# A gated cross-attention and expert block: gate moved to ScalarE and GpSimd, similarity steps in PSUM, first batch in a group of its own, loops unrolled

## The chip, the cores and the metric

The kernel runs on 1 core of one Trainium2 chip. The metric is the device time of one execution in microseconds (us). The time before is 257.56 us, the median of 3 runs (257.23 to 257.66). In this text PE is the matmul engine TensorE, PEld its weight loads, DVE is VectorE, ACT is ScalarE, POOL is GpSimd and SP is the engine that issues the transfers. L700 is line 700 of the kernel before.

## The reference, cut to what matters

```python
# x, ctx: (16, 128, 1024); weight: (128, 128, 3); router_w (8, 1024); A (8, 16, 1024); Bm (8, 1024, 16)
def xattn(feature, embedding, weight):            # per batch: C = 128 channels, T = 1024
    emb_l = pad(embedding[:, :, :-1], left=1); emb_r = pad(embedding[:, :, 1:], right=1)
    sim = stack([cos(embedding, emb_l), cos(embedding, embedding), cos(embedding, emb_r)], axis=1)
    att = repeat(sim, C, axis=1)                  # (B, 3*C, T)
    inp = stack([f_pad[:, :, k:k + T] for k in range(3)], axis=2).reshape(B, C * 3, T)
    return einsum('bit,oi->bot', inp * att, weight.reshape(O, C * 3))
def ffn(x, router_w, router_b, A, Bm):            # x as 2048 rows of 1024
    probs = softmax(x @ router_w.T + router_b)    # 8 experts, the best 2 are kept
    topv, topi = top_k(probs, 2); gates = topv / sum(topv)
    h = einsum('nd,erd->ner', x, A)               # 16 hidden values per expert
    return einsum('ner,eor->no', h * w[:, :, None], Bm) * 0.5     # w: gates at topi
x = x + tanh(g_xattn) * xattn(layernorm(x), ctx, weight)
x = x + tanh(g_ffn) * ffn(layernorm(x), router_w, router_b, A, Bm)
```

## The kernel before

A batch is a tile of 128 partitions by 1024 columns; there are 16. Each goes through this pipeline, and each engine has a program of its own, written out by hand and tied to the others by semaphores. An engine executes its program strictly in order.

**The similarities, per group of four batches.** For each `ctx` batch ACT squares it (L461) and DVE or POOL multiplies neighbouring columns (L708, L343). `sum_context` (L920) sums both over the partitions with a one-hot weight, one PSUM row set per batch of the group. When four batches are in, ACT copies the sums out (L467), PE turns them round (`transpose_context`, L927), and DVE runs a chain of small instructions on 128 x 32 values: `context_columns` (L625, L627), the inverse square root by three Newton steps in `inverse_norms` (L636 to L648), the products in `similarities` (L658 to L666; PE's `next_norms`, L934, gives the neighbour's norm) and the split into three bf16 parts in `split_similarities` (L672 to L684). All of these operands lie in SBUF, apart from the two that PE has just written. PE turns the parts into rows (L941), and ACT copies them to `rows` (L471, L476). The chain for group g + 1 is dealt out, instruction by instruction, between the other DVE work of group g.

**The convolution, per batch in six steps.** A step i is a half h = i // 3 of the columns and a tap k = i % 3. PE spreads the similarity over the channels (`spread_similarities`, L953, banks 0 and 1 in turn), DVE multiplies it with the normalized feature (`modulate`, L700, result `pt`), and the tap is multiplied with its weights into bank 2 or 3. There are two ways to do this. A *split* tap has ACT round `pt` to `pt_hi` (L507) and POOL compute `pt_lo` (L368), and PE makes three fp32r matmuls (L969 to L971). A *whole* tap has PE make an fp32 matmul of `pt` itself, two instructions in the trace (L965). Whole are all six of the first batch and four of the 24 of each group (`WHOLE`), so there are 22 whole and 74 split taps. `LEAD` = 2: spreading runs four steps and modulation two steps ahead of the tap.

**The expert part.** DVE adds x (`residual`, L716), takes statistics (L722, L731), and POOL makes the inverse deviation (L394, L396). PE transposes the result (L980), multiplies with the expert weights (`experts_in`, L995), ACT copies hidden values and logits to SBUF (L527). DVE computes the logit (L740), the eight largest and their places (L744, L748), the distance to the largest (L747), and, after an exponential on ACT (L520), the gate in five instructions (L755, L758, L764, L768, L773, a batch later). POOL scales the hidden values (L377), PE transposes them (L1004), ACT makes two copies (L534, L535), POOL the remainder (L388), PE multiplies with the output weights (`experts_out`, L1014 to L1018, through one bank), DVE adds (`finish`, L780), and SP stores.

**The loops.** The body is one group of four batches. Each engine runs it for the first group, then twice in a hardware loop, then for the last group. Ahead of the first tap stand the four `sum_context` of group 0 and one whole similarity chain.

```python
WHOLE = ((), (4,), (4,), (3, 4))
LEAD = 2
...
                    for i in range(6):
                        if not (last and j + (i + 2 + LEAD) // 6 == G):
                            spread_similarities(*shifted(g, j, i, 2 + LEAD))
...
                        tap(g, j, i)
```

## Time and profile before

| what | value |
|---|---|
| time, median of 3 runs | 257.56 us (257.23 to 257.66) |
| span of the profiled execution | 256.0 us |
| time outside that span, by the three runs | 1.2 to 1.7 us (median run: 1.56 us) |
| PE, DVE, ACT, POOL busy | 216.1, 213.1, 157.2, 155.2 us |
| mean granted TensorE clock | 0.933 of full speed |

The profiled execution has no time of its own beside its span; what lies around the span is taken from the timed runs. An engine is busy while an instruction of it runs; a busy PE counts matmuls that overlap once. The granted clock is the share of the full 2.4 GHz at which PE ran.

### The profile page before, as it was taken

To read this page: it belongs to the slowest core of one execution; us is meant where nothing else is said; L and a number is where in the kernel's file an instruction comes from. 1 tells how busy PE (TensorE), PEld (TensorE's weight loads), DVE (VectorE), ACT (ScalarE), POOL (GpSimd) and SP (SyncE) were. 2 spreads that over 40 slices of the span, in tenths; PEclk is the share of its full clock that TensorE was granted. 3 is DMA by queue.
4 is the path that set the end of the run, shared out by engine and by line. 5 is a ranking of instruction groups with operands and counts; after the bars stand their busy time and mean duration, and the time that the engine had idled before them with its cause. 6 is when DMAs were issued, how large, how long until landed. Compare 5 with 4: busy or idle time off the path is not lost.

```text
span 256.0 us, 4267 instructions
## 1 busy us (share of the span) xinstructions
PE 216.1 (84%) x1080; PEld 136.3 (53%) x1080; DVE 213.1 (83%) x481; ACT 157.2 (61%) x283; POOL 155.2 (61%) x225
## 2 busy tenths in 40 slices
PE   6755999976995999896995999996998979697983
PEld 5133236554763546574753546573756656565761
DVE  2545686999989899999789899999789996979674
ACT  3668749664676678753686778753587765533320
POOL 2014558939376998846276998846267956745321
PEclk9996599998899999996899999996799988989999
DMA  6999106151221307171220304031222202020206
GB/s 205 333 293 387 59 0 188 63 186 64 82 82 21 147 0 292 40 286 43 82 86 10 154 0 154 10 105 59 82 82 81 83 1 83 3 82 0 82 3 247
DMA packets 8769, 27.24 MB, mean 106 GB/s; under 512 B 1616, under 2 KB 2128, under 8 KB 8752
## 3 DMA queue, kind: packets, MB, share of 16 engines
q1 hardware_dynamic: 8752, 27.05, 29.2%
q8 instruction: 7, 0.11, 0.2%
q14 instruction: 10, 0.08, 0.1%
HBM read 18.65 MB, written 8.39 MB: 106 GB/s over the span
## 4 chain that ended last, share of the span: by engine, by line
DVE 38%; PE 24%; issue 20%; POOL 7%; ACT 5%; DMA 2%; DVEq 1%; SPq 0%; ACTq 0%; POOLq 0%
DVE pt L700 7%; DVE pick L755 4%; DVE logit L740 4%; PE bank L965 4%; PE bank L995 3%; DVE bn L722 3%; PE bank L920 3%; POOL pt_lo L368 3%; DMA et<-ctx 2%; DVE below L747 2%; PE bank L980 2%; DVE x L716 2%; PE bank L953 2%; DVE pr L708 2%; POOL rs L396 2%
## 5 line engine op out<-in xcount | busy, mean ns | idle before, releaser
L368 POOL TENSOR_TENSOR pt_lo<-pt,pt_hi 128x512 fp32r<-128x512 f32 x74 | 96.3, 1304 | 33.2 <-ACT pt_hi L507 25.0
L700 DVE TENSOR_TENSOR pt<-xn,bank 128x512 f32<-128x512 f32 x96 | 64.9, 679 | 12.1 <-PE bank L953 6.9
L507 ACT ACTIVATE pt_hi<-pt 128x512 fp32r<-128x512 f32 x74 | 46.3, 627 | 36.1 <-DVE pt L700 35.6
L953 PE MATMUL bank<-rows,sel 96*128 96x512 bf16 (+1 forms) x96 | 39.6, 414 | 13.2 <-DVE pt L700 12.0
L969 PE MATMUL bank<-pt_hi,w_hi 128*128 128x512 f32 x74 | 37.1, 502 | 0.0
L995 PE MATMUL bank<-aT,xT 128*128 128x136 f32 x256 | 35.8, 284 | 0.0
L513 ACT ACTIVATE xT<-bank 128x512 f32<-128x512 f32 x32 | 18.9, 591 | 26.4 <-PE bank L980 26.4
L953 PEld LDWEIGHTS bank<-rows,sel 96*128 96x128 bf16 x96 | 9.5, 100 | 46.3 <-DVE pt L700 23.4
L995 PEld LDWEIGHTS bank<-aT,xT 128*128 128x128 f32 x256 | 33.5, 193 | 0.9 <-ACT xT L513 0.4
L970 PE MATMUL bank<-pt_lo,w_hi 128*128 128x512 f32 x74 | 30.3, 410 | 0.0
L971 PE MATMUL bank<-pt_hi,w_lo 128*128 128x512 f32 x74 | 30.2, 408 | 0.0
L980 PE MATMUL bank<-ident,x 128*128 128x128 f32 x128 | 21.2, 291 | 7.7 <-DVE x L716 7.7
L716 DVE TENSOR_TENSOR x<-bank,xt 128x512 f32<-128x512 f32 x32 | 22.0, 688 | 4.9 <-PE bank L971 4.2
L965 PE MATMUL bank<-pt,wT 128*128 128x512 f32 x44 | 25.9, 675 | 0.0
L980 PEld LDWEIGHTS bank<-ident,x 128*128 128x128 f32 x128 | 16.2, 149 | 14.5 <-DVE x L716 10.0
L920 PE MATMUL bank<-sq,onehot 128*32 128x512 f32 x64 | 20.8, 746 | 1.8 <-DVE pr L708 1.8
L780 DVE TENSOR_TENSOR x<-bank,x 128x512 f32<-128x512 f32 x32 | 21.2, 666 | 0.9 <-PE bank L1018 0.7
L489 ACT ACTIVATE unread<-xt,minus_mean 128x1024 f32<-128x1024 f32 x16 | 18.4, 1148 | 5.6 <-POOL minus_mean L348 5.6
L722 DVE BATCH_NORM_STATS2 bn<-x 128x6 f32<-128x512 f32 x32 | 21.7, 677 | 0.0
L920 PE MATMUL bank<-pr,onehot 128*32 128x512 f32 x64 | 20.8, 747 | 0.0
L461 ACT ACTIVATE sq<-et 128x1024 f32<-128x1024 f32 x16 | 16.8, 1048 | 5.9 <-DMA et<-ctx 4.9
L498 ACT ACTIVATE xn<-xt,offset,rs 128x1024 f32<-128x1024 f32 x16 | 19.7, 1229 | 0.6 <-POOL offset L359 0.6
(100 smaller groups left out, 386.3 us busy)
## 6 DMA issues: line engine op xcount, KB each, us to landing
et<-ctx SPq DMA_DIRECT2D x16, 512.0 KB, 5.8
xt<-x SPq DMA_DIRECT2D x16, 512.0 KB, 3.3
out<-x SPq DMA_DIRECT2D x15, 512.0 KB, 2.6
aT_in<-expert_aT SPq DMA_DIRECT2D x1, 544.0 KB, 9.4
bm_in<-expert_b SPq DMA_DIRECT2D x1, 512.0 KB, 9.9
out<-x SPq DMA_DIRECT2D x2, 256.0 KB, 2.0
sel<-select SPq DMA_DIRECT2D x1, 288.0 KB, 10.5
wT_in<-conv_wT SPq DMA_DIRECT2D x1, 192.0 KB, 10.0
```

The costliest lines, as they stand in the source:

```text
L368: nc.gpsimd.tensor_tensor(pt_lo[:, i, :], pt[:, i, :], pt_hi[:, i, :], ALU.subtract).then_inc(lo_done, 1)
L507: nc.scalar.activation(pt_hi[:, i, :], pt[:, i, :], ACT.Copy).then_inc(hi_done, 1)
L700: nc.vector.tensor_tensor(pt[:, i, :], xn[:, j % 2, h * HALF + k:(h + 1) * HALF + k], sim_ps[i % 2][:, :], ALU.mult).then_inc(mod_done, 1)
L722: nc.vector.bn_stats(bn2[:, j % 2, 6 * h:6 * h + 6], x1[:, j, half(h)]).then_inc(bn2_done, 1)
L920: last = nc.tensor.matmul(sum_ps[32 * q:32 * q + 32, :], onehot[:, j, :], src[:, j % 2, half(q % 2)], start=(j == 0), stop=(j == G - 1))
L953: nc.tensor.matmul(sim_ps[i % 2][:, :], sel[:, j, k, :], rows[:, g, half(h)], start=True, stop=True).then_inc(spread, 1)
L965: nc.tensor.matmul(conv_ps[h][:, :], wT[:, k * P:(k + 1) * P], pt[:, i, :], start=(k == 0), stop=(k == TAPS - 1)).then_inc(tap_done, 1)
L969: nc.tensor.matmul(conv_ps[h][:, :], w_hi[:, k, :], pt_hi[:, i, :], start=(k == 0), stop=False)
L970: nc.tensor.matmul(conv_ps[h][:, :], w_hi[:, k, :], pt_lo[:, i, :], start=False, stop=False)
L971: nc.tensor.matmul(conv_ps[h][:, :], w_lo[:, k, :], pt_hi[:, i, :], start=False, stop=(k == TAPS - 1)).then_inc(tap_done, 1)
L980: last = nc.tensor.transpose(xT_ps[:, c * P:(c + 1) * P], x1[:, j, h * HALF + c * P:h * HALF + (c + 1) * P], ident[:, :])
L995: last = nc.tensor.matmul(h_ps, xT[:, j % 2, c, :], aT[:, c, :], start=(c == 0), stop=(c == KC - 1))
```

## The change

Nearly every function is rewritten, and the loops over groups are unrolled into a loop over the batches n = 0 to 15 at build time. What an engine does in step (n, i) is now read from tables. The parts:

1. **Gate.** The exponential, the distance and the five DVE instructions go. ACT computes the second weight as sigmoid(second - first) from the two largest logits (`second_weight`). POOL builds the gate in six small instructions (`weigh_experts`). The logit reads its main operand from PSUM rather than from the copy in SBUF. The copy `hwT` goes (one ACT instruction), and the remainder `hwT_lo` moves from POOL to DVE with one PSUM operand; the transposed hidden values lie in the output bank.
2. **Similarity chain.** The chain's long-lived values stay in free columns of the PSUM bank that holds the turned sums; guess, rinv, dr and the bf16 parts remain in SBUF. The copy L625 goes. The order of the four sums in the bank changes to suit.
3. **Groups** are (0), (1, 2, 3), then three of four. So there are five chains instead of four. Group 1's chain is run in batch 0. Loads are reordered: x 0 comes before ctx 1.
4. **Lead.** Modulation is three steps and spreading five steps ahead of the tap, from batch 1 on (one and three in batch 0).
5. **Taps.** In each batch from 1 on, steps 2 and 5 are whole, the other four split: 36 whole and 60 split in all.
6. **Small moves.** The mean is scaled in the ACT instruction that sums (POOL's L348 goes). `rows` 0 to 63 are copied by DVE in every group. Products: eight on DVE, eight on POOL (ten and six before).

```diff
-WHOLE = ((), (4,), (4,), (3, 4))
-LEAD = 2
+WHOLE = (2, 5)
+GROUPS = ((0,), (1, 2, 3), (4, 5, 6, 7), (8, 9, 10, 11), (12, 13, 14, 15))
+TURNS = {(1, 3): 2, (5, 3): 3, (9, 3): 4}
+NEIGHBOURS = {(0, 2): 1, (2, 3): 2, (6, 3): 3, (10, 3): 4}
+ROWS = {(0, 3): 1, (3, 0): 2, (7, 0): 3, (11, 0): 4}
+ON_POOL = (2, 3, 5, 7, 9, 11, 13, 15)
...
+        def ahead(m):
+            lead = 3 if m >= STEPS else 2 if m == STEPS - 1 else 1
+            return min(m + lead, M - 1)
...
+            def weigh_experts(n):                                    # POOL
+                i = n % 2
...
+                pool.wait_ge(topi_done, n + 1)
+                nc.gpsimd.tensor_copy(topf[:, i, :], topi[:, i, 0:2]).then_inc(topf_done, 1)
+                pool.wait_ge(w2_done, n + 1)
+                nc.gpsimd.tensor_tensor(g2[:, i:i + 1], w2[:, i:i + 1], rs2[:, i:i + 1], ALU.mult).then_inc(g2_done, 1)
+                pool.wait_ge(g2_done, n + 1)
+                nc.gpsimd.tensor_tensor(g1[:, i:i + 1], rs2[:, i:i + 1], g2[:, i:i + 1], ALU.subtract).then_inc(g1_done, 1)
+                pool.wait_ge(topf_done, n + 1)
+                nc.gpsimd.tensor_scalar(gb[:, i, :], ids[:, :], topf[:, i, 1:2], g2[:, i:i + 1], ALU.is_equal,
+                                        ALU.mult).then_inc(picked, 1)
+                pool.wait_ge(g1_done, n + 1)
+                nc.gpsimd.tensor_scalar(ga[:, i, :], ids[:, :], topf[:, i, 0:1], g1[:, i:i + 1], ALU.is_equal,
+                                        ALU.mult).then_inc(picked, 1)
+                pool.wait_ge(picked, 2 * (n + 1))
+                nc.gpsimd.tensor_tensor(gate[:, i, :], ga[:, i, :], gb[:, i, :], ALU.add).then_inc(gate_done, 1)
...
+            def second_weight(n):                                    # ACT
+                nc.scalar.activation(w2[:, i:i + 1], top[:, i, 0:1], ACT.Sigmoid, bias=top[:, i, 1:2],
+                                     scale=-1.0).then_inc(w2_done, 1)
...
+            def inverse_norms(q):                                    # DVE
+                s = columns(q)                                       # the PSUM bank of the sums
+                n_all, guess_n, excess = s[:, :, 4:8], s[:, :, 8:12], s[:, :, 12:16]
...
-                nc.vector.scalar_tensor_tensor(out=logit[:, :], in0=hs[:, j % 2, ER:ER + E],
-                                               scalar=rs2[:, j % 2:j % 2 + 1], in1=rb[:, :],
+                nc.vector.scalar_tensor_tensor(out=logit[:, i, :], in0=h_ps[:, ER:ER + E], scalar=rs2[:, i:i + 1],
+                                               in1=rb[:, :], op0=ALU.mult, op1=ALU.add).then_inc(logit_done, 1)
...
+            def hidden_rest(n):                                      # now DVE
+                nc.vector.tensor_tensor(hwT_lo[:, i, :], hwT_ps(n), hwT_hi[:, i, :].bitcast(F32),
+                                        ALU.subtract).then_inc(hwT_rest, 1)
...
+            sum_context(0)                                           # PE, ahead of the loop
+            transpose_context(0)
+            sum_context(1)
+            next_norms(0)
+            sum_context(2)
             transpose_similarities(0)
+            sum_context(3)
+            for k in steps_at(-1, 2):
+                spread_similarities(k)
+            transpose_context(1)
+            for n in range(B):
+                for i in range(STEPS):
+                    if (n, i) in ROWS:
+                        transpose_similarities(ROWS[n, i])
+                    for k in steps_at(m, 2):
+                        spread_similarities(k)
+                    if i == 0 and n >= 3:
+                        experts_out(n - 3, 0)
+                    if i == 1 and n >= 1:
+                        transpose_tokens(n - 1, 1)
+                    if i == 2 and n >= 1:
+                        experts_in(n - 1, 0)
+                    if i == 2 and n >= 3:
+                        experts_out(n - 3, 1)
+                    if i == 3 and n >= 1:
+                        experts_in(n - 1, 1)
+                    if i == 4 and n >= 2:
+                        transpose_hidden(n - 2)
+                    if i == 5:
+                        transpose_tokens(n, 0)
...
+                    tap(m)
```

## Rows read from the trace of the kernel before

**Rows 1.** The page: span, and busy time of each engine.

```profile
span 256.0 us, 4267 instructions
PE 216.1 (84%) x1080; PEld 136.3 (53%) x1080; DVE 213.1 (83%) x481; ACT 157.2 (61%) x283; POOL 155.2 (61%) x225
```

**Rows 2.** Windows: stretch, length, busy per engine, clock, DMA share, GB/s.

```profile
36.00:244.00 208.00, 182.56 (x936) 120.36 (x932) 187.14 (x420) 133.00 (x247) 141.33 (x191) 0.94 0.23 84
120.00:124.00 4.00, 4.00 (x13) 2.81 (x12) 2.77 (x12) 1.11 (x2) 0.17 (x1) 0.50 0.00 0
```

**Rows 3.** Waits: who waited for whom; us in total, times, longest.

```profile
PEld bank L953 <- DVE pt L700: 23.4, 26, 3.1
PE bank L934 <- DVE rinv L648: 8.4, 4, 2.2
```

**Rows 4.** Timeline: start, us, engine, line; one stretch of POOL and DVE.

```profile
92.50 1.29 POOL L368 TENSOR_TENSOR pt_lo<-pt,pt_hi 128x512 fp32r<-128x512 f32 x1
92.76 1.07 DVE L755 TENSOR_SCALAR pick<-ids,topi 128x8 f32<-128x8 f32 x1
```

**Rows 5.** Single lines of DVE: ns minimum/median/maximum, first and last start.

```profile
L740 DVE SCALAR_TENSOR_TENSOR logit<-hs,rs,rb x16: 215/980/1234, 45.3 to 247.2; 128x8 f32<-128x8 f32 x16
L700 DVE TENSOR_TENSOR pt<-xn,bank x96: 660/678/689, 24.7 to 237.2; 128x512 f32<-128x512 f32 x96
```

**Rows 6.** Groups of instructions: busy us, mean ns; then idle before.

```profile
L740 DVE SCALAR_TENSOR_TENSOR logit<-hs,rs,rb 128x8 f32<-128x8 f32 x16 | 12.8, 801 | 8.1 <-ACT hs L527 6.5 <-POOL rs L396 1.4
L755 DVE TENSOR_SCALAR pick<-ids,topi 128x8 f32<-128x8 f32 x16 | 12.3, 767 | 0.0
L747 DVE TENSOR_SCALAR below<-logit,top 128x8 f32<-128x8 f32 x16 | 8.4, 522 | 0.1
L773 DVE TENSOR_SCALAR gate<-expk,einv,rs 128x8 f32<-128x8 f32 x16 | 7.6, 474 | 0.0
L758 DVE SCALAR_TENSOR_TENSOR pick<-ids,topi,pick 128x8 f32<-128x8 f32 x16 | 6.6, 413 | 0.5
L764 DVE SCALAR_TENSOR_TENSOR expk<-expo,pick 128x8 f32<-128x8 f32 x16 | 5.4, 339 | 0.0
L648 DVE SCALAR_TENSOR_TENSOR rinv<-excess,guess 128x32 f32<-128x32 f32 x4 | 3.8, 961 | 0.0
L662 DVE TENSOR_TENSOR sim<-dr,bank 128x64 f32<-128x64 f32 x4 | 0.9, 220 | 0.6 <-PE bank L935 0.5
L708 DVE TENSOR_TENSOR pr<-et 128x1023 f32<-128x1023 f32 x10 | 14.1, 1408 | 6.5 <-DMA et<-ctx 5.6 <-PE bank L920 0.8
```

**Rows 7.** The chain that ended last: start, us, PE's pieces back to back.

```profile
238.12 0.93 PE bank L995 x8
239.04 0.23 PE bank L969
...
239.85 1.77 PE bank L965 x4
...
242.33 0.44 PE bank L980 x4
```

**Rows 8.** Windows 36 to 244, matmuls of L920 alone: PE and PEld busy.

```profile
sum 208.00, PE 10.73 PEld 1.57; mean PE 10.73 PEld 1.57
```

**Rows 9.** The chain that ended last: start, us, the stretch before batch 0.

```profile
9.04 5.38 PE bank L920 x24
...
24.68 0.70 DVE pt L700
```

**Rows 10.** Timeline of DVE: the residual's second half of batches 0 and 15.

```profile
39.02 0.69 DVE L716 TENSOR_TENSOR x<-bank,xt 128x512 f32<-128x512 f32 x1
...
243.49 0.69 DVE L716 TENSOR_TENSOR x<-bank,xt 128x512 f32<-128x512 f32 x1 [1.56 <-PE bank L971]
```

**Rows 11.** Groups of instructions of POOL and ACT, as rows 6.

```profile
L368 POOL TENSOR_TENSOR pt_lo<-pt,pt_hi 128x512 fp32r<-128x512 f32 x74 | 96.3, 1304 | 33.2 <-ACT pt_hi L507 25.0 <-PE bank L971 8.0
L507 ACT ACTIVATE pt_hi<-pt 128x512 fp32r<-128x512 f32 x74 | 46.3, 627 | 36.1 <-DVE pt L700 35.6
L348 POOL TENSOR_TENSOR minus_mean<-xsum,minus_t 128x1 f32<-128x1 f32 x16 | 3.7, 232 | 11.9 <-ACT unread L483 11.9
L461 ACT ACT_TABLE_LOAD x1 | 1.3, 1283 | 0.7 <-PEq L1140 0.7
```

More of the change, by code:

```diff
@@ L29, in flamingo_kernel @@
     B, C, T = x.shape
-    NG = B // G
     KC = T // P
@@ L238, in parts_before, with whole, parts_up_to @@
-        def parts_before(g, j, i):
-            count = [6 - len(steps) for steps in WHOLE]
-            return sum(count) * g + sum(count[:j]) - count[0] + sum(m not in WHOLE[j] for m in range(i))
-        def past(g, j, k):
-            return not isinstance(g, int) or G * g + j >= k
+        SETUP = 11
         def half(h):
             return slice(h * HALF, (h + 1) * HALF)
+        def whole(k):
+            return k < STEPS or k % STEPS in WHOLE
+        def parts_up_to(k):
+            return sum(not whole(m) for m in range(k + 1))
@@ L316, in _ @@
+            for n in range(B - 4, B - 1):
+                store(n)
             for h in range(2):
@@ L440, in body @@
                                                 ALU.subtract).then_inc(bm_lo_done, 1)
[L441 to L453 removed]
+            weigh_experts(B - 2)
@@ L593, in body @@
                         nc.scalar.activation(bm_hi[:, :], bm[:, :], ACT.Copy).then_inc(bm_hi_done, 1)
-                    high(3)
-                    if one:
-                        logits_evacuate(*before(1))
-                    high(4)
-                    if two:
-                        hidden_evacuate(*before(2))
-                    if stats:
-                        feature_squares(*ahead)
-                    if j == 1 and not last:
-                        sums_evacuate(g + 1)
-                    high(5)
@@ L605, in body @@
-                    if j == 0 and not last:
-                        square(g + 1, 2)
-                    if one:
-                        exponent(*before(1))
-                    tokens_evacuate(g, j, 0)
-            each_group(act, body)
-            tokens_evacuate(NG - 1, G - 1, 1)
-            logits_evacuate(NG - 1, G - 1)
-            hidden_evacuate(NG - 1, G - 2, last_hwT_ps[0])
-            exponent(NG - 1, G - 1)
-            hidden_evacuate(NG - 1, G - 1, last_hwT_ps[1])
+                    if i == 5:
+                        tokens_evacuate(n, 0)
@@ L781, in finish, with some @@
                                         ALU.add).then_inc(out_done, 1)
+            def some(of, count):
+                for _ in range(count):
+                    next(of, None)
             nc.vector.memset(rows[64:96, :, 0:1], 0.0).then_inc(setup, 1)
-            dve.wait_ge(setup, 11)
-            for j in range(G):
-                next_product(0, j)
-            context_columns(0)
+            dve.wait_ge(setup, SETUP)
+            product(0)
+            product(1)
             for _ in inverse_norms(0):
@@ L871, in body @@
-                    residual(g, j, 0)
-                    steps(roots)
-                    steps(picks)
-                    steps(roots)
-                    ahead(5)
-                    steps(roots)
-                    steps(picks)
-                    steps(roots)
-                    token_stats(g, j, 0)
-                    if j == 2 and not last:
-                        similarities(g + 1)
-                        parts = split_similarities(g + 1)
-                        steps(parts)
@@ new lines, in _ @@
+                    some(norms, 1)
+                    some(sims, 1)
+                    if i == 3:
+                        residual(n, 0)
+                    if i == 5 and n >= 2:
+                        hidden_rest(n - 2)
+                    if i == 5:
+                        some(picks, 1)
+                    if i == 4:
+                        token_stats(n, 0)
+                    if i == 5:
+                        some(norms, 1)
+                        some(picks, 1)
+                        some(sims, 1)
+                        some(picks, 1)
@@ L1098 @@
+            experts_out(B - 3, 0)
+            transpose_tokens(B - 1, 1)
+            experts_in(B - 1, 0)
+            experts_out(B - 3, 1)
+            experts_in(B - 1, 1)
+            transpose_hidden(B - 2)
+            experts_out(B - 2, 0)
+            experts_out(B - 2, 1)
+            transpose_hidden(B - 1)
+            experts_out(B - 1, 0)
+            experts_out(B - 1, 1)
 def kernel(x, ctx_4096, g_xattn, g_ffn, L0_xattn_weight, L0_ffn_router_w, L0_ffn_router_b, L0_ffn_A, L0_ffn_Bm):
```

1073 lines of the change are left out of this document (458 added, 615 removed).

## The prediction

> **What bounds the kernel now.** I read four views. The page's first lines say which engines can matter at all: PE and DVE are both busy for more than 210 of 256.0 us, ACT and POOL for some 155 [rows 1]. That doesn't separate PE from DVE, so I took the steady stretch, windows 36 to 244: DVE 187.1, PE 182.6 of 208 us [rows 2]. Then the waits: the entries of PE there name DVE, its multiplication L700 above all, and at the group's end the last Newton step L648 [rows 3]. So PE waits for DVE. Part of PE's busy time is also no work: in the windows there are stretches such as 120 to 124 at a clock of 0.50, the lower of the two levels (1.2 GHz), and the mean is 0.94 [rows 2]. That one comes after PE had waited for L648.
>
> The last view tells why DVE is full. The timeline shows the 128x8 comparison L755 start at 92.76 and end at 93.83, while POOL's L368 runs from 92.50 to 93.79 [rows 4]: eight columns take a microsecond because the instruction ends only when POOL's has. The single lines say the same of L740 (215 ns at best, 980 at the median), but not of L700, which has one operand in PSUM and stays within 660 to 689 in 96 executions, although POOL runs L368 under most of them [rows 5]. So DVE's small instructions with SBUF operands are held by POOL, and those with a PSUM operand aren't.
>
> The steady part runs from the second residual of batch 0 (39.0) to that of batch 15 (243.5): 204.5 us, 13.6 per batch. 12.5 us follow it [rows 10].
>
> **Step 1, DVE's work.** The gate's lines that go cost 12.3 + 8.4 + 7.6 + 6.6 + 5.4 = 40.3 us [rows 6]. The logit stays, with PSUM as its main operand: 12.8 falls to 16 x 0.215 = 3.4, so 9.4 less [rows 5, 6]. The chain's L648 falls from 3.8 to 4 x 0.22 = 0.9 by the PSUM row L662, 2.9 less; its other held instructions I leave out. Two products fewer: 2.8 less [rows 6]. Added: `hidden_rest`, 128 columns with a PSUM operand, lies between L662 (0.22, 64 columns) and L700 (0.68, 512 columns); I take 0.3, near the first, 16 times: 4.8 (ends 3.5 and 10.9). A fifth chain of some 22 small instructions at 0.22: 4.8. Four more copies of `rows`, each taken as one L700: 2.7. Sum: 213.1 - 55.4 + 12.3 = 170 us. Of the 43 us some 40 lie in the steady part: 147 instead of 187, 9.8 per batch.
>
> The Trainium skill (SBUF: State Buffer, "Who interferes with whom") says that VectorE and GpSimd share a port pair as an exclusive lock, and that a VectorE instruction with at most one SBUF input, outside the two-port modes, doesn't take it. By that rule the two rows on L755 and L740 are the lock, and the new chain and gate are free of it. It doesn't say whether the per-partition scalar of the logit counts as an input.
>
> I bound that from rows: if the logit is held as before, DVE keeps the 9.4 us and stands at 179, still under PE.
>
> **Step 2, PE's work.** At full clock, pieces back to back are: one 512-column fp32r pass 0.23, a whole tap 1.77 / 2 = 0.89, half of `experts_in` 0.93, four token transposes 0.44 [rows 7]. Per batch from 1 on: six spreads 1.4, four split taps 12 x 0.23 = 2.8, two whole taps 1.8, `experts_in` 1.9, `experts_out` 1.4, transposes 0.9 and 0.1: 10.3 us. Fifteen batches: 155. Ten `sum_context` of 10.73 / 10 each [rows 8] add 10.7; three groups' turns, each about three times the four transposes, add 4. Together 170 us, 11.3 per batch. By the same prices the old mix (74 split, 16 whole taps) is 166: the change costs PE 4 us, since a whole tap takes 0.89 against 0.69.
>
> So PE had 166 us of work at full clock in 204.5: 38.5 us were waits and slow clock. With DVE at 9.8 and PE at 11.3 per batch, PE is the bound. Of the 38.5 the waits on DVE and the slow stretches behind them should mostly go; the deeper lead (three steps instead of two) helps as well, since a split tap passes DVE, ACT and POOL (0.68 + 0.63 + 1.30, [rows 5, 11]) within three steps of 1.9 us. I keep a quarter, 10 us: PE's program still depends on DVE's residual and additions twice per batch. Ends: nothing kept, or two thirds (25). Steady part: 170 + 10 = 180 us.
>
> **Step 3, POOL and ACT.** POOL: 14 fewer `pt_lo` are -18.3, six small gate instructions 16 times at the 0.232 of L348 are +22.3 [rows 11]: 155.2 becomes 159, at most 10 per batch; the six are covered by PE's 11.3. ACT: 14 fewer `pt_hi` at 0.627, -8.8; one small sigmoid against one exponential. Both hidden. Unrolling alone I cost at nothing; no row prices it.
>
> **Step 4, the start.** With batch 0 alone in its group the first chain need not wait for the other three `sum_context`, which now end at 9.04 + 5.38 = 14.4 [rows 9]. But DVE takes product 1 first, whose load now comes behind x 0, and PE's list puts `sum_context` 1, 2 and 3 between the chain's stages; number 3 waits for an ACT square that stands behind the copy of `rows`. Of the 4.2 us that could be won (a start of the chain near 10.2) I keep 1: the first modulation near 23.7 instead of 24.68 [rows 9]. Batch 0 then contains group 1's whole chain, and its taps 3 to 5 wait for it; but its taps are no slower than now. I put its second residual at 37.5 instead of 39.0; ends: 34.8 (all 4.2 won) and 43 (chain of 22 x 0.22 = 5 us uncovered). The end after batch 15 keeps its 12.5: the gate there is a serial chain on POOL rather than DVE, 0 to 1 us longer.
>
> **Sum.** 37.5 + 180 + 12.5 = 230 us of span against 256.0. The runs' median lies 1.56 above the profiled span, so 231.5 us.
>
> **Rivals.**
> - *A, in-order coupling (0.20).* DVE, ACT and POOL have room, but their programs and PE's wait for each other at fixed places: the one output bank is now also used for the transposed hidden values, so `transpose_hidden` waits for an addition on DVE one and a half steps after its matmuls. Then more than half of the 38.5 stays, 20 to 27 us: 241 to 249. For it: now too DVE isn't full (187 of 208). Against: the waits name DVE.
> - *B, POOL's gate becomes the bound, slower (0.04).* The trace shows no comparison with two per-partition scalars on POOL. The nearest rows are L348 (0.23) and L368 (1.30), the ends. POOL has 8.5 us per batch without the six; it reaches today's 13.6 if each takes 0.85. At 1.0 the steady part is 15 x 14.5 = 217, the time 269. Everything behind them on POOL, `hidden` and the next `pt_lo`, is late, and PE waits for `pt_lo`.
> - *C, sigmoid reloads tables (0.03).* One table load of 1.28 us serves the whole kernel now [rows 11]. If the sigmoid needs another table than the copies around it, there are two loads per batch: 41 us on ACT, 157 - 9 + 41 = 189, and its bursts delay `pt_hi`: some 240 to 260.
> - *D, the DVE relief isn't the limit (0.03).* All 38.5 stays: 37.5 + 170 + 38.5 + 12.5 + 1.56 = 260.
>
> On C, the Trainium skill (ScalarE: Activation LUTs, "Table sets: the hidden batching unit") says that tanh is in the sigmoid's set too and that cheap functions are in every set; by that there is one load or two in all. Its price for a switch is 2.66 us with the drain, by which two switches per batch would cost 85 us on ACT, an estimate, and the kernel would be slower. The one load seen for tanh, exponential and copies agrees as far as it goes.
>
> **Chances and range.** The forecast, steady part kept to between 0 and 18 us above PE's sum, has 0.70: 221 to 240. The range goes from 221 to 245 and takes in the nearer half of A; outside are its rest, B, D, part of C and a better start. Slower by over 0.2% is B, D and a part of C, 0.06; within 0.2%, about what a measurement here can tell from no change, 0.01; faster 0.93.
>
> **What would show it.** Right: L740's successor near 0.22 us in all executions; DVE busy near 170; 15 batches in about 180 us; the clock above 0.96; PE over 90% busy in the steady part. Wrong: POOL's six instructions above 0.5 us each, more than two table loads, PE waits for `hwT_rest` or the output bank, or the first modulation after 25 us. The prediction falls if PE's idle and slow time stays above 25 us.

## The result, and the profile after

The changed kernel takes 261.15 us (median of 4 runs, 259.4 to 261.96) against 257.39 us for the kernel before beside it. The ratio is 1.0173, 95% interval 1.0104 to 1.0242: slower, by 4 us. The forecast was 231.5 us, so it missed by 30 us and had the wrong sign. The runs of one kernel differ by up to 3%, so all ratios here, and the column "undisturbed" of the table further down, leave out each run that lies more than some 1.5% above the fastest of its kernel. In this part L-numbers without a word are those of the changed kernel.

First the page of the changed kernel, against [rows 1].

```profile
span 260.0 us, 3722 instructions
PE 215.1 (83%) x1082; PEld 135.8 (52%) x1082; DVE 167.3 (64%) x403; ACT 144.5 (56%) x253; POOL 155.2 (60%) x277
```

DVE lost 45.8 us of work (170 us were forecast, 167.3 came), and yet the span grew. Next the groups of instructions that answer to [rows 6, 11]: busy us, mean ns.

```profile
L676 DVE SCALAR_TENSOR_TENSOR logit<-bank,rs,rb 128x8 f32<-128x8 f32 x16 | 3.5, 217 | 0.0
L593 DVE TENSOR_TENSOR bank<-bank,guess 128x32 f32<-128x32 f32 x15 | 3.0, 198 | 0.4
L691 DVE TENSOR_TENSOR hwT_lo<-bank,hwT_hi 128x128 fp32r<-128x128 f32 x16 | 4.6, 285 | 2.5 <-ACT hwT_hi L505 2.4
L379 POOL TENSOR_SCALAR gb<-ids,topf,g 128x8 f32<-128x8 f32 x16 | 8.5, 533 | 0.0
L382 POOL TENSOR_SCALAR ga<-ids,topf,g 128x8 f32<-128x8 f32 x16 | 6.3, 393 | 0.0
L497 ACT ACT_TABLE_LOAD x1 | 1.3, 1283 | 0.0
```

The prices of the instructions came out as forecast: the logit and the chain are held no more, the remainder costs 0.285 us, POOL's comparisons are in the mean below the 0.85 us at which they would matter (two single executions of L379 took 1.44 us), and the sigmoid loads its table once. So the loss isn't in what the instructions cost. The windows, against [rows 2]: the steady part from the second residual of batch 0 to that of batch 15, its last four batches, and a stretch of low clock.

```profile
49.50:246.30 196.80, 174.99 (x908) 114.75 (x907) 137.61 (x329) 117.44 (x214) 136.72 (x234) 0.97 0.27 89
205.70:246.30 40.60, 39.84 (x209) 28.56 (x208) 31.16 (x69) 22.76 (x46) 29.71 (x58) 1.00 0.22 78
121.00:124.00 3.00, 2.96 (x8) 1.55 (x8) 2.13 (x12) 1.40 (x3) 1.00 (x5) 0.50 0.02 5
```

The last four batches take 10.15 us each with PE 98% busy at full clock; PE's prices had said 10.3. The steady part as a whole takes 196.8 us where 180 were forecast, and it begins at 49.5 where 37.5 were (timeline of DVE, the rows that answer to [rows 10]):

```profile
49.50 0.69 DVE L659 TENSOR_TENSOR x<-bank,xt 128x512 f32<-128x512 f32 x1 [0.23 <-PE bank L841]
...
246.27 0.69 DVE L659 TENSOR_TENSOR x<-bank,xt 128x512 f32<-128x512 f32 x1 [0.79 <-PE bank L841]
```

So of the 29.6 us that were missed the start has 12.0, the steady part 16.8 and the tail 1.2 (260.0 - 246.3 = 13.7 against 12.5); the profiled execution lies 0.4 above the median. Against the kernel before, the sign has two parts: the steady part is 7.7 us shorter (196.8 against 204.5), but the start, which now holds two chains instead of one, is 10.5 us longer (49.5 against 39.0) and the tail 1.2, together the 4.0 us by which the spans differ. With the start of before the kernel would have been faster by some 6 us, an estimate from these rows. Where the steady part's went, the waits say (in total, times, longest), against [rows 3]:

```profile
PEld bank L827 <- DVE pt L652: 49.1, 63, 3.7
PE bank L827 <- DVE pt L652: 24.7, 25, 2.2
...
DVE bank L616 <- PE bank L809: 18.5, 5, 5.5
...
DVE bank L581 <- PE bank L802: 16.4, 5, 5.9
...
DVE rows L639 <- PE bank L815: 10.0, 5, 2.9
...
DVE x L659 <- DMA out<-x: 4.0, 3, 3.4
```

PE still waits for DVE's multiplications, although DVE is busy for only 137.6 of the 196.8 us. And DVE waits for PE at three places of the similarity chain, five times each, once per chain: 45 us together, 32 of them in the chains of groups 2 to 4 (the timeline of each). Of such waits the kernel before had this one (waits, before), beside some below 1.3 us:

```profile
DVE nd L625 <- PE bank L927: 3.6, 1, 3.6
```

One chain, first on DVE and then on PE (timelines), shows how the two belong together:

```profile
116.47 0.20 DVE L581 TENSOR_SCALAR bank<-bank 128x32 f32<-128x32 f32 x1 [4.68 <-PE bank L802]
...
131.97 0.23 DVE L616 TENSOR_TENSOR bank<-dr,bank 128x64 f32<-128x64 f32 x1 [3.82 <-PE bank L809]
139.21 0.68 DVE L639 COPY rows<-bank 64x1024 bf16<-64x1024 bf16 x1 [2.14 <-PE bank L815]
```

```profile
119.06 0.39 PE L827 MATMUL bank<-rows,sel 96*128 96x512 bf16 x1 [1.92 <-DVE pt L652]
121.04 0.61 PE L827 MATMUL bank<-rows,sel 96*128 96x512 bf16 x1 [0.78 <-DVE pt L652]
...
134.20 0.39 PE L827 MATMUL bank<-rows,sel 96*128 96x512 bf16 x1 [1.49 <-DVE pt L652]
...
140.55 0.39 PE L827 MATMUL bank<-rows,sel 96*128 96x512 bf16 x1 [1.37 <-DVE pt L652]
```

PE spreads two steps ahead of DVE's multiplication, so a DVE that isn't full can get up to two steps of its program ahead of PE's. At L581 it needs the sums that PE turns in the same step of its program, and stands 4.68 us, since it can't pass over that instruction. Its multiplications for the next taps stand behind it, so when it goes on it is level with PE, and now PE waits for it: PE stands for 1.92 us until 119.06, then for 0.78, and the clock falls to 0.50 in the windows (121 to 124: the lower level, 1.2 GHz). From second residual to second residual, the six batches in which DVE reads a result of PE (1, 2, 5, 6, 9, 10) take 15.0 to 16.7 us. Without chains and with the store ahead of the loads (run b3 below) they take 9.6 to 12.4. Batches 3, 7 and 11 to 14 take 10.5 to 10.8 in both. Batches 4 and 8 are longer for another reason: PE makes three `sum_context` in each, and they take 13.7 us in b3 as well.

The last wait of the list is another thing. The diff has one line of SyncE's program that the prediction passed over as "loads are reordered":

```diff
 # batch n of SyncE's program: load_x(n + 3), loads of ctx, then
-  store(n - 3)
+  store(n - 4)
```

SyncE's timeline, and DVE's with the second addition of batch 0 (L696), after which the store could go, and the first residual of batch 4 (L659), which needs the buffer:

```profile
82.28 11.14 SPq L274 DMA_DIRECT2D xt<-x  x2
93.52 1.20 SPq L269 DMA_DIRECT2D et<-ctx  x2
94.77 0.42 SPq L278 DMA_DIRECT2D out<-x  x1
```

```profile
87.53 0.68 DVE L696 TENSOR_TENSOR x<-bank,x 128x512 f32<-128x512 f32 x1
...
102.53 0.69 DVE L659 TENSOR_TENSOR x<-bank,xt 128x512 f32<-128x512 f32 x1 [3.44 <-DMA out<-x]
```

The data was ready at 88.2. The store went out at 94.8, behind a load of x that waited for the residual of batch 3 (the second of the two in the first line; by itself it starts at 93.10), and behind two ctx loads, and DVE stood for it 3.44 us.

### The profile page after: what moved, and what is told of

Its sections match the earlier page's. It is cut to its first block, busy times and chain, and to the rows that moved or that the text cites. A ratio compares the mean times of both kernels' runs of the same rounds, so it can differ in the third digit from the quotient of the medians.

```text
span 260.0 us, 3722 instructions
## 1 busy us (share of the span) xinstructions
PE 215.1 (83%) x1082; PEld 135.8 (52%) x1082; DVE 167.3 (64%) x403; ACT 144.5 (56%) x253; POOL 155.2 (60%) x277
## 4 chain that ended last, share of the span: by engine, by line
PE 55%; DVE 18%; issue 10%; DMA 8%; POOL 4%; ACT 2%; SPq 0%; POOLq 0%; DVEq 0%; ACTq 0%
PE bank L841 11%; PE bank L866 10%; DVE pt L652 7%; PE bank L827 7%; DMA out<-x 6%; PE bank L855 4%; PE bank L795 4%; PE bank L845 3%; PE bank L846 3%; PE bank L847 3%; DVE bn L664 2%; DMA xt<-x 2%; PE bank L884 2%; PE bank L885 2%; PE bank L886 2%
## 5 line engine op out<-in xcount | busy, mean ns | idle before, releaser
L357 POOL TENSOR_TENSOR pt_lo<-pt,pt_hi 128x512 fp32r<-128x512 f32 x60 | 76.9, 1283 | 52.6 <-ACT pt_hi L478 52.4
L652 DVE TENSOR_TENSOR pt<-xn,bank 128x512 f32<-128x512 f32 x96 | 63.7, 669 | 6.1 <-PE bank L827 5.3
L478 ACT ACTIVATE pt_hi<-pt 128x512 fp32r<-128x512 f32 x60 | 37.5, 627 | 50.6 <-DVE pt L652 50.5
L827 PE MATMUL bank<-rows,sel 96*128 96x512 bf16 x96 | 39.3, 414 | 24.8 <-DVE pt L652 24.7
L841 PE MATMUL bank<-pt,wT 128*128 128x512 f32 x72 | 42.7, 679 | 0.0
L659 DVE TENSOR_TENSOR x<-bank,xt 128x512 f32<-128x512 f32 x32 | 22.0, 687 | 14.8 <-PE bank L841 10.7
L696 DVE TENSOR_TENSOR x<-bank,x 128x512 f32<-128x512 f32 x32 | 21.8, 680 | 11.5 <-PE bank L886 11.5
L845 PE MATMUL bank<-pt_hi,w_hi 128*128 128x512 f32 x60 | 28.4, 474 | 0.0
L795 PE MATMUL bank<-sq,onehot 128*32 128x512 f32 x64 | 19.7, 694 | 6.3 <-ACT sq L438 3.1
L846 PE MATMUL bank<-pt_lo,w_hi 128*128 128x512 f32 x60 | 24.0, 400 | 0.0
L847 PE MATMUL bank<-pt_hi,w_lo 128*128 128x512 f32 x60 | 23.9, 399 | 0.0
L344 POOL TENSOR_TENSOR ve<-squares,eps_t 128x1 f32<-128x1 f32 x16 | 4.2, 260 | 27.8 <-ACT unread L462 27.8
```

The costliest lines, as they stand in the source:

```text
L357: nc.gpsimd.tensor_tensor(pt_lo[:, i, :], pt[:, i, :], pt_hi[:, i, :], ALU.subtract).then_inc(lo_done, 1)
L478: nc.scalar.activation(pt_hi[:, i, :], pt[:, i, :], ACT.Copy).then_inc(hi_done, 1)
L652: nc.vector.tensor_tensor(pt[:, i, :], xn[:, n % 2, h * HALF + t:(h + 1) * HALF + t], sim_ps[k % 2][:, :], ALU.mult).then_inc(mod_done, 1)
L795: last = nc.tensor.matmul(sum_ps(q)[32 * r:32 * r + 32, :], onehot[:, b, :], src[:, :, r // 2, :], start=(b == 0), stop=(b == len(GROUPS[q ...
L827: nc.tensor.matmul(sim_ps[k % 2][:, :], sel[:, SLOT_OF[n], t, :], rows[:, q % 2, half(h)], start=True, stop=True).then_inc(spread, 1)
L841: nc.tensor.matmul(conv_ps[h][:, :], wT[:, t * P:(t + 1) * P], pt[:, i, :], start=(t == 0), stop=(t == TAPS - 1)).then_inc(tap_done, 1)
```

## The experiments

The table holds what all runs are compared by. "Start" is the begin of the second residual of batch 0, "steady" the time from there to that of batch 15, both from the timeline of DVE in the profiled execution (kernel before: [rows 10]). That execution is a single one, and its time stands beside them. "All" and "undisturbed" are medians; the last column has the ratio to the kernel before, with its 95% interval. Runs whose names begin with the same letter were made on the same chip, each letter's on another. The kernel before took 255.16, 255.28, 254.93 and 254.36 us (undisturbed) beside a, b, c and d, and 257.39 us (all) beside the changed kernel. The ratios differ from the quotients of these medians by up to 1.4%, so differences of a few us are read here from the undisturbed times, and across chips they carry an error of 1 to 2 us.

| kernel | start | steady | profiled | all | undisturbed (runs) | ratio |
|---|---|---|---|---|---|---|
| before | 39.0 | 204.5 | | 257.39 | | |
| changed | 49.5 | 196.8 | 261.57 | 261.15 | 261.15 (4) | 1.017 (1.010 to 1.024) |
| a1_norms_later | 48.5 | 189.9 | 254.65 | 255.88 | 250.59 (1) | |
| a2_all_later | 50.8 | 182.2 | 249.49 | 247.11 | 245.07 (2) | 0.954 (0.944 to 0.963) |
| a3_no_chain | 51.0 | 172.8 | 239.75 | 238.63 | 234.11 (1) | |
| a4_start | 42.4 | 196.0 | 253.70 | 253.14 | 253.14 (4) | 0.982 (0.972 to 0.991) |
| b1_store | 49.7 | 191.1 | 256.02 | 257.34 | 257.34 (9) | 1.008 (1.004 to 1.012) |
| b2_later_store | 50.5 | 176.7 | 242.51 | 241.11 | 241.11 (4) | 0.940 (0.934 to 0.946) |
| b3_no_chain_store | 49.4 | 165.4 | 230.07 | 230.09 | 230.09 (4) | 0.899 (0.893 to 0.905) |
| b4_later_store_start | 47.2 | 176.1 | 238.56 | 234.66 | 233.74 (5) | 0.916 (0.910 to 0.921) |
| c1_before_no_gate | 38.3 | 182.8 | 234.77 | 235.74 | 235.05 (4) | 0.924 (0.918 to 0.930) |
| c2_lead_two | 42.1 | 176.5 | 233.94 | 235.86 | 235.86 (5) | 0.926 (0.921 to 0.932) |
| c3_one_whole | 41.8 | 176.9 | 234.01 | 234.38 | 234.13 (3) | 0.920 (0.914 to 0.927) |
| c4_warm | 43.8 | 176.3 | 235.36 | 235.99 | 234.22 (3) | 0.916 (0.909 to 0.923) |
| d1_loads | 42.1 | 176.4 | 234.98 | 234.45 | 234.45 (4) | 0.909 (0.897 to 0.921) |
| d2_no_gate_late_store | 39.6 | 190.3 | 243.68 | 240.94 | 239.04 (2) | 0.931 (0.916 to 0.946) |
| d3_before_late_store | 39.5 | 208.9 | 262.67 | 260.90 | 257.95 (3) | 1.014 (1.003 to 1.025) |

**The handoffs (a1, a2, a3).** a1 starts DVE's part of the chain two steps later than PE turns the sums; a2 does the same at the two other places.

```diff
 # a1, DVE
 TURNS = {(1, 3): 2, (5, 3): 3, (9, 3): 4}                  # PE turns the sums; DVE no longer starts here
+NORMS_FROM = {(1, 5): 2, (5, 5): 3, (9, 5): 4}             # DVE alone
 # a2, besides
-NEIGHBOURS = {(0, 2): 1, (2, 3): 2, (6, 3): 3, (10, 3): 4}
+NEIGHBOURS = {(0, 2): 1, (2, 2): 2, (6, 2): 3, (10, 2): 4}   # PE
+SIMS_FROM  = {(0, 2): 1, (2, 4): 2, (6, 4): 3, (10, 4): 4}   # DVE
-ROWS = {(0, 3): 1, (3, 0): 2, (7, 0): 3, (11, 0): 4}
+ROWS = {(0, 3): 1, (2, 5): 2, (6, 5): 3, (10, 5): 4}         # PE
+ROWS_REST = {(0, 3): 1, (3, 1): 2, (7, 1): 3, (11, 1): 4}    # DVE; ACT at (3, 0), (7, 0), (11, 0)
 # a3
-TURNS = {...}; NEIGHBOURS = {(0, 2): 1, ...}; ROWS = {(0, 3): 1, ...}
+TURNS = {};    NEIGHBOURS = {(0, 2): 1};      ROWS = {(0, 3): 1}
```

Expected of a1:

> The changed kernel, but DVE begins the norm chain of groups 2 to 4 two steps after PE has turned the sums, rather than in the same step. Handoff theory (DVE runs ahead of PE, meets PE's result of the same step, stands still and loses its lead): the wait of some 5 us in front of the first chain instruction goes in three groups, 10 to 15 us less than 261, that is 246 to 251. Rival, the chain's own work on DVE and PE makes these batches long: no change, 259 to 262. Rival, the split of the taps, the gate on POOL or the deeper lead make them long: no change.

Expected of a2:

> As before, and the other two handoffs of groups 2 to 4 get room as well: PE makes the neighbour norms one step earlier and DVE begins the similarities two steps after that; PE turns the parts round one step earlier, ACT copies its rows one step and DVE its rows two steps after that. No work is left out. Handoff theory: the nine batches that now last 15.6 us fall to 12 or less, 225 to 235. Rival, the chain's own work: 255 to 262. Rival, taps, gate or lead: 255 to 262.

Expected of a3:

> The changed kernel without the similarity chains of groups 2 to 4 (turn, norms, neighbour norms, splitting, rows are left out; the batches 4 to 15 use rows left by the groups 0 and 1; sums over the context are still made). It bounds what chain and handoffs together can cost. Handoff theory: nine batches fall from 15.6 to about 11 us, 215 to 225, and the kernel with later handoffs comes within 10 us of it. Rival, the chain's own work: also 215 to 225, but far from the kernel with later handoffs. Rival, taps, gate or lead: stays above 245.

The direction is as the handoff theory said, the size isn't. The same work takes 6.9 us less in the steady part with one handoff moved, 14.6 with three; without the chains of groups 2 to 4 it takes 24.0 less. (The profiled executions of these three lie above the undisturbed times; b1 against b2 below, both within 1.4 us of theirs, gives the 14.4 us of the three handoffs again.) The four runs of a1 go from 250.59 to 257.3, so only the fastest lies in the theory's range. a2 is 16 us below the changed kernel by the undisturbed runs, and still above the range; so is a3, of which no run is below 234. DVE's waits in a2 (L620 and L643 there are L616 and L639 of the changed kernel; L700 is the addition, L663 the residual):

```profile
DVE x L700 <- PE bank L892: 20.4, 17, 2.2
...
DVE bank L620 <- PE bank L815: 9.4, 2, 6.5
DVE x L663 <- DMA out<-x: 7.1, 3, 3.9
...
DVE rows L643 <- PE bank L821: 3.7, 2, 2.9
```

The chain's waits of the three later groups are gone; only the two early chains have theirs. DVE's other waits for PE, at the addition, are those of an engine with time to spare. But the waits for stores grew, from 4.0 to 7.1 us here and 10.1 in a3, where batches 4 and 5 took 16.1 and 15.5 us without a chain. There was a second limit behind the first.

**The start (a4).** On PE, the chain's rows stand ahead of `sum_context(2)` and the first two spreads of batch 0 ahead of `sum_context(3)`, `expert_means` goes from step 1 of batch 0 to step 4, and `next_norms` ahead of `sum_context` in a step.

```diff
-sum_context(2); transpose_similarities(0); sum_context(3); spreads of steps 0 to 2
+transpose_similarities(0); sum_context(2); spreads 0 and 1; sum_context(3); spread 2
-if n == 0 and i == 1: expert_means()
+if n == 0 and i == 4: expert_means()
```

> The changed kernel with another order at the start only: on PE the parts of group 0 are turned round before the sums of context 2, two spreads stand before the sums of context 3, the expert means are made in step 4 of batch 0 instead of step 1 (the subtraction on DVE moves to batch 1), and the neighbour norms stand before the sums of the same step. Theory that the start lost its time to PE work placed in front of what DVE waits for: first modulation from 24.8 to about 20, second residual of batch 0 from 49.5 to 41 to 44, 5 to 8 us less in all, 253 to 256. Rival, the start is set by transfers: within 1 us of the changed kernel.

It came at 253.14: 8 us below the changed kernel, with the start at 42.4 instead of 49.5 and the steady part unchanged (196.0). The first multiplication, in the changed kernel and in this one (timeline of DVE, one fence each):

```profile
24.81 1.29 DVE L652 TENSOR_TENSOR pt<-xn,bank 128x512 f32<-128x512 f32 x2 [4.05 <-PE bank L827]
```

```profile
21.19 1.29 DVE L652 TENSOR_TENSOR pt<-xn,bank 128x512 f32<-128x512 f32 x2 [1.79 <-PE bank L827]
```

3.6 us are won there, and 3.4 more within batch 0, where group 1's chain waited 5.49 us at L616 in the changed kernel and 2.12 here. The clock isn't what made this start late: in b3, whose program is the same up to here, it was granted 1.00 in the window 9 to 25, against 0.50 in the changed kernel, and the second residual of batch 0 came at 49.4 all the same.

**The store (b1 to b4).** The store is put ahead of the loads: in the changed kernel (b1), in a2 (b2), in a3 (b3), and in a2 with a4's start (b4).

```diff
 for n in range(1, B):
+    if n >= 4: store(n - 4)
     if n + 3 < B: load_x(n + 3)
     ...                                        # loads of ctx
-    if n >= 4: store(n - 4)
```

> The changed kernel with one thing put back as before: SyncE issues the store of a finished batch ahead of the next load of x and of the ctx loads, instead of behind them (one batch later). In the profile of the changed kernel the residual L659 waited 4.0 us for stores, three times, the longest 3.4 at 102.5. Theory of the store: those waits go, and what PE lost behind them, 3 to 6 us in all: 255 to 258. Rival, that the similarity handoffs alone set the slow batches, so that the store's wait only moves to the next handoff: 259 to 262, with the same nine batches of some 15.6 us.

> The kernel with all handoffs a few steps later (247.1 us), with the store put back ahead of the loads. Its profile shows 7.1 us of waits of the residual for stores, three times, up to 3.9. Two limits in turn (theory now): with the handoffs moved the store is the next that holds DVE; taken away it gives 7 us and some of the lead lost behind each: 236 to 241. Rival, handoffs alone: the waits move elsewhere, 245 to 249. By both the start stays as it is, second residual of batch 0 near 50.5.

> The kernel without the chains of groups 2 to 4 (238.6 us; its output isn't the reference's), with the store put back ahead of the loads. Its profile still had slow batches: 16.1 and 15.5 us for batches 4 and 5, with 10.1 us of waits for stores. Theory (the store is the second limit): all batches from 3 on take 10.5 to 11, the second residual of batch 15 comes near 213, the time is 226 to 231. Rival (what is left is PE's own pace or the slow clock): 236 to 239.

> All three together: handoffs later, the store ahead of the loads, and PE's start put in another order (spreads of batch 0 ahead of two sums, the expert means three steps later). The start alone gave 8 us of 261. If the three add: 228 to 234, faster than the kernel before by 9 to 11%. If the start's gain is eaten because batch 0 and 1 wait for loads instead: 236 to 241.

All four medians fell within 0.7 us of the ranges of the theory of two limits, and outside the rivals'; for b1 that is weak, as its 257.34 lies only 2 us below the rival's range and its chip was the quicker by as much. The steady part shrinks by 5.7, 5.5 and 7.4 us (changed to b1, a2 to b2, a3 to b3; a2 and a3 by profiled executions that lie 4 to 6 us high), the undisturbed times by 3.8, 4.0 and 4.0, and no wait for a store is left in any of the four. The issues in the changed kernel and in b1 (KB each, median us from issue to landing, one fence each):

```profile
out<-x SPq DMA_DIRECT2D x15, 512.0 KB, 5.0
```

```profile
out<-x SPq DMA_DIRECT2D x15, 512.0 KB, 2.6
```

The store isn't only issued later in the changed kernel, it also takes twice as long to land when it goes out right behind the loads: the median is 4.9 us in a2, d2 and d3 too, and 2.6 in before, b2 and c1. In b3, where neither holds, this is what the steady batches are like (windows, 82 to 214):

```profile
82.00:214.00 132.00, 130.21 (x694) 86.38 (x693) 102.29 (x215) 86.28 (x163) 107.34 (x188) 1.00 0.27 100
```

PE is 99% busy at full clock. Its steady part, 165.4 us, is what step 2 had summed for PE less the three groups' turns that b3 leaves out: 170 - 4 = 166.

**DVE's relief by itself (c1).** The kernel before, with the gate's instructions left out of DVE. Schedule, store, lead, taps and chain are those of before.

```diff
-below = logit - top[0]; topi = max_index(...); pick0, pick, expk, esum, einv    # L747, L748, L755 to L768
-gate = expk * einv * rs2
+gate = ids * rs2
```

> The kernel before with the gate left out (output isn't the reference's): the largest's place L748, L747, L755, L758, L764, L768 and ACT's exponential go, and the gate is the expert numbers times the inverse deviation. DVE loses 12.3 + 8.4 + 6.6 + 5.4 + 1.3 + 2.4 + 2.5 + 1.3 = 40.2 of its 213.1 us; chain, lead, taps, groups and the store's place stay as before. What the prediction's step 2 said (DVE's relief alone gives back most of the 38.5 us of waits and slow clock): 228 to 234. Theory now (relief gives what DVE really held, and the chain's handoffs, where DVE arrives early, keep a part): 238 to 247. Rival D (DVE isn't the limit): 253 to 257.

235.74 us (235.05 undisturbed), a ratio of 0.924; the steady part goes from 204.5 to 182.8. That lies between the 228 to 234 of the prediction's step 2 and the theory's 238 to 247. Rival D is refuted: DVE was the limit, and relieving it in the old order is worth 20 us. The chain's handoffs cost little in the old order. DVE's waits for PE in it are short (L622 and L659 are the chain's first two places; L776 is the copy of `rows` ahead of batch 0, the only one that DVE makes there):

```profile
DVE nd L622 <- PE bank L908: 4.3, 3, 2.7
DVE sim L659 <- PE bank L916: 2.9, 1, 2.9
...
DVE rows L776 <- PE bank L922: 1.2, 1, 1.2
```

8.4 us in four chains, against 45 in the changed kernel's five. The programs say why. In the kernel before, PE turns the sums in step 5 of the group's second batch and DVE reads them in step 1 of the third, two steps later. PE makes the neighbour norms in step 4 and DVE reads them at the end of step 5. The rows of the later groups are copied by ACT alone. The change gave up these distances: its tables put each pair into one step, and DVE copies rows too. What the same-step order costs beside a full DVE was not run.

**Lead, mix of taps, clock, loads (c2, c3, c4, d1).** Each is b4 with one thing changed.

```diff
 # c2
-lead = 3 if m >= STEPS else 2 if m == STEPS - 1 else 1
+lead = 2 if m >= STEPS - 1 else 1
 # c3
-WHOLE = (2, 5)
+WHOLE = (5,)
 # c4, PE: 7 and 6 matmuls of 128 columns whose result isn't used, around the first next_norms
+for _ in range(7): matmul(conv_ps[0][:, 0:P], mean_w, mean_w)
 # d1, SyncE: selection matrix and weights ahead of ctx 2
-load_e(2); sel; wT
+sel; wT; load_e(2)
```

> The kernel with handoffs later, store and start (234.7 us), with a lead of two steps instead of three. If the third step of lead is what lets PE ride over DVE's stalls and the way of a split tap through DVE, ACT and POOL (0.67 + 0.63 + 1.28 us and the handoffs, within two steps of 1.75): 238 to 246. If two steps are enough: 233.5 to 236.

> The same kernel with one whole tap per batch from 1 on instead of two (15 more split taps): PE has 15 x 0.2 = 3 us less to do, ACT 15 x 0.63 = 9.4 and POOL 15 x 1.28 = 19.2 more (POOL 174 us, 10.9 per batch). If PE's work sets the pace: 231 to 232.5. If POOL's queue does, so that the mix of taps is part of the gain: 236 to 241.

> The same kernel with 13 idle matmuls (128 columns, results not used) on PE where it waits in the start: seven behind sum_context(1), six behind the first next_norms. In its profile the clock was at the lower level from 15 us on, the three sums in the start took 1.87 us each instead of 1.06, and the second residual of batch 0 came at 47.2, in the kernel with the start alone at 42.4. If the clock in the start is what differs: 43 or below, and 229 to 232 us. If the start waits on DVE's chain and on loads anyway: 234 to 236.

> The kernel with handoffs later, store and start (234.7 us), with the loads of the selection matrix and of the weights issued ahead of ctx 2. In its profile PE waited for the selection matrix until 14.5 us, and its second residual of batch 0 came at 47.2, in like kernels at 42 to 44. If the load is the rest of the start's delay: the first modulation 1 to 2 us earlier than 20.3 to 21.2, the second residual at 40 to 42, 232 to 234 us. If ctx 2, which now comes later, takes its place: 234 to 236.

None of the four does much: 234.1 to 235.9 us undisturbed against 233.7, steady parts within 0.8 us of each other. So the third step of lead is worth 2 us at most, and nothing in the steady part. The mix of taps is a wash within 0.8 us of the steady part: batches 12 to 14 take 10.4 us each with one whole tap against 10.5 with two, and the batches before them differ either way. The idle matmuls don't help. The start of b4 in its profile (47.2) was not that of its kind: a4, with the same program up to there, has 42.4, and c2, c3, c4 and d1, with nearly the same, have 41.8 to 43.8. The profiled execution of b4 is also 4.8 us above its kernel's undisturbed median. The windows 30 to 50 of b4 and of c2 show the granted clock at 0.67 and 0.95:

```profile
30.00:50.00 20.00, 18.28 (x76) 8.59 (x75) 11.06 (x20) 8.85 (x12) 9.19 (x8) 0.67 0.06 19
```

```profile
30.00:50.00 20.00, 18.07 (x102) 9.06 (x102) 12.63 (x23) 13.28 (x19) 11.89 (x11) 0.95 0.22 80
```

What decides that clock I can't say; c4 didn't settle it.

**The store's place by itself (d2, d3).** The kernels c1 and before, with the store one batch later as in the changed kernel.

```diff
-if j >= 3: store(g, j - 3)
-elif not first: store(g - 1, j + 1)
+if not first: store(g - 1, j)
```

> The kernel before with the gate left out (235.7 us; output isn't the reference's), with the store of a finished batch issued one batch later, behind the next load of x and the ctx loads, as in the changed kernel. There the store was issued 2.3 us after the first half's residual of the batch before, and the next residual wanted its buffer some 8 us later. If the store's place costs whenever the batches are short: waits of L713 for stores appear, 237.5 to 243. If only the changed kernel's own order (residual at step 3, its addition just ahead of it) makes it late: 234.5 to 236.5, no wait.

> The kernel before with the store's place alone moved one batch later. A batch takes 13.6 us there and the residual's first half comes some 9 us after the second half of the batch before. If a late store is hidden by a full DVE: 254.5 to 256.5, no change. If it costs on its own: 258 to 261.

Both theories that hid it were wrong: d2 239.04 against 235.05 of c1 (undisturbed, on two chips), d3 257.95 against 254.36 of before on the same chip, ratio 1.014 with an interval that excludes 1. The steady parts are 7.5 and 4.4 us longer, but both profiled executions are 4.6 us or more above their undisturbed medians, so the times are the better measure. The wait for stores appears in both; first d2, then d3:

```profile
DVE x L711 <- DMA out<-x: 4.5, 2, 2.7
```

```profile
DVE x L714 <- DMA out<-x: 5.5, 2, 3.5
```

The late store costs about 4 us even with a full DVE (d3). A likely reason, not tested apart: a full DVE is itself the limit, so a wait in its program is lost.

## Why the prediction was wrong, point by point

**Step 1, DVE's work: right.** 170 us forecast, 167.3 measured. The logit takes 217 ns in the mean and never more than 226, although in eight of its 16 executions POOL was in the middle of a 1.28 us `pt_lo` (L357); the Newton steps' L593 takes 198 ns. By the rule in the Trainium skill (SBUF — State Buffer, "Who interferes with whom"), cited there, VectorE instructions with at most one SBUF input, outside the two-port modes, don't take the lock; the rows agree. The logit has two SBUF operands beside the one in PSUM, a per-partition scalar and the bias row, so in this trace neither of them led to its being held.

**Step 3, POOL and ACT: right.** POOL 155.2 us (159 forecast), though partly by luck: the comparisons with two scalars took 0.39 and 0.53 us in the mean instead of 0.23, two more products were added, and the sum had forgotten that the remainder and the mean's scaling leave POOL. Rivals B and C are out: no bound on POOL, one table load for the sigmoid, two in all.

**Step 2, PE's work: the sum was right, what was kept of the waits was wrong.** PE's 170 us hold: b3 gives 165.4 without the turns. (One figure beside it was off: 14 taps more at 0.20 us each are 2.8 us, not 4.) The failed step is "I keep a quarter, 10 us". The changed kernel kept 196.8 - 170 = 27 us, above the 25 at which the prediction said it would fall. The runs show what the 27 are:

- 5.7 us the store's place (changed against b1). By the undisturbed times it is about 4 us, in this pair (3.8, across chips) as in a2 to b2, a3 to b3 and c1 to d2 (4.0 each) and in before to d3, on one chip (3.6). The prediction had the line in front of it and gave it no price.
- 14.4 us the three handoffs of the chain (b1 against b2, both on one chip; changed against a2 gives 14.6).
- What is left is 176.7 - 170 = 6.7 us (b2). That is what the forecast's 10 us stood for, and with both repaired they would have been enough. All of it is tied to the chains of groups 2 to 4, since b3, which lacks them, stands at its price.

Step 2's premise, that DVE's relief gives the waits back, was right in direction where it was made, and short in size: in the old order the relief is worth 21.7 us of the steady part (c1), where the forecast wanted back 28.5 of its 38.5. What it lacked was the question what the relieved engine would do in the new order. The table of steps has PE's turning and DVE's first use of it in the same step (1, 3), and likewise at the two other places. A DVE with room gets ahead of PE's program, by up to two steps, and then stands at a same-step handoff until PE has come up. In the old order, with one or two steps between PE's instruction and DVE's, a light DVE waits 8.4 us in all (c1); in the new one 45. Most of what the relief had gained in the steady part was paid back there and at the store.

**Step 2's lead: not borne out.** "The deeper lead helps as well": c2 shows nothing in the steady part and 2 us at most in the time.

**Step 4, the start: the second failed step, wrong by 12.0 us.** 37.5 forecast, 49.5 measured, above its upper end of 43. What failed is "but its taps are no slower than now", with group 1's chain priced as 5 us of DVE's small instructions and nothing for what DVE and PE wait for each other in it. The first multiplication came at 24.81 (23.7 forecast), so 1.1 us of it lie before. The rest lies in batch 0: its first tap starts as in the kernel before (27.24 us, before 27.22), its last at 48.43 against 37.96 (timelines of PE). a4 gives back 7.1 us, half of them by PE's order before batch 0 and half by the order within it. One cause was in the diff and missed: `expert_means` stood in PE's waits before batch 0 (2.3 us in two pieces) and now stands in batch 0's step 1 (3.15 us), with group 1's `next_norms` behind it. The other 4.9 us, down to 37.5, stay open; neither loads (d1) nor idle matmuls (c4) moved them.

**Rivals.** A had the right kind (engines that wait for each other at fixed places) and the wrong place: not the output bank or the residual, but the chain, and so the wrong price, 241 to 249. D had the right number, 260, by luck and for a wrong reason: the relief does count (c1), its gain went elsewhere. No rival said that a relieved engine in front of a handoff can lose again what its relief gains, and none had the start later than before.

The ledger in times: 261.15 to 233.74 us by the three repairs of b4, the work unchanged, 8.4% under the kernel before (ratio 0.916). 2 us above the forecast are left.

## What to carry to other kernels

When an engine that was full is relieved, look for each instruction on it that waits for another engine's result of the same step: it can now arrive early, stand, and lose the lead that the others live on. Give such handoffs as many steps as the engine can run ahead (two here, which took the waits away in a2 and b2), and look in the diff for distances that the old order had. Price the start by itself: here it turned a shorter steady part into a longer kernel. And read every line of the transfer queue's program in a diff: a store that moves behind a load inherits the load's wait, and the buffer it frees is late by as much.

## What the runs showed of the hardware

A store of 512 KB issued right behind loads landed after 5.0 us in the median, issued ahead of them after 2.6, in the same kernel (changed and b1).

Kernels with nearly the same start were granted 0.67 (b4) or 0.95 (c2) of the full clock in windows 30 to 50, and the second residual of batch 0 came 5 us apart; which of the two a run gets wasn't explained.

Two comparisons of the same form on POOL (128x8, two per-partition scalars, L379 and L382) took 533 and 393 ns in the mean, but 403 and 394 in the median. The whole difference is two executions of L379 that took 1.44 us, at 96.09 and 154.91. Both began within 0.01 us of a product on DVE (L573, 128x1023, both operands in SBUF, 1.24 us) and ended 0.2 us after it. So here POOL's small instruction was the one that was held, as DVE's L755 was in [rows 4].
